# Products that nobody reads, in TensorE's waits between the phases of a two-layer kernel and in its last step

## The reference

```
xa = layer_norm(x);  sx = previous token - this token
xxx = tanh((xa + sx * maa_x) @ maa_w1), then five small products with maa_w2
xk, xw, xv, xr, xg = xa + sx * (maa_stack + xxx)
w = exp(-exp(time_decay + tanh(xw @ td_w1) @ td_w2))
r, k, v = xr @ Wr.T, xk @ Wk.T, xv @ Wv.T;  g = silu(xg @ Wg.T)
per token and head: out = r . (u * k v^T + s);  s = k v^T + w * s
x1 = x + group_norm(out) * g @ Wo.T
xc = layer_norm(x1), shifted and mixed into xk2 and xr2
result = x1 + sigmoid(xr2 @ Wfr.T) * (square(relu(xk2 @ Wfk.T)) @ Wfv.T)
```

## Time and profile before

| | before |
|---|---|
| median of three runs | 1484.47 us |
| the profiled execution, its own time | 1483.6 us |
| its span, first to last instruction | 1481.8 us |
| mean clock granted to TensorE | 0.973 of full speed |
| TensorE busy | 1388.5 us (94%) |
| VectorE busy | 888.9 us (60%) |
| ScalarE busy | 722.5 us (49%) |
| GpSimd busy | 486.7 us (33%) |

### The profile page before, as it was taken

One profiled execution on the slowest core, in us unless ns is written; L12 is line 12 of the kernel. 1 busy time (PEld: TensorE's weight loads), 2 busy tenths in 40 slices (PEclk: granted clock), 3 DMA queues, 4 the chain that ended last, 5 costly groups with the idle time before them and its releaser, 6 DMA issues. The chain is left out here.

```text
span 1481.8 us, 41201 instructions
## 1 busy us (share of the span) xinstructions
PE 1388.5 (94%) x16448; PEld 1007.6 (68%) x16448; DVE 888.9 (60%) x2287; ACT 722.5 (49%) x1772; POOL 486.7 (33%) x530
## 2 busy tenths in 40 slices
PE   5999999999999999947989999999999999999965
PEld 4777777777777777626766667666676666666632
DVE  3444444444444443433887788887878878787751
ACT  3666666666666666521245344443444434444422
POOL 2211111111111111011543456434554345543330
PEclk9999999999999999968899999999999999999997
DMA  7531111111111100012001000011000010010000
GB/s 217 152 92 41 41 41 40 39 39 39 39 38 35 34 24 14 7 32 105 11 20 27 27 20 9 25 26 26 19 10 26 26 27 8 20 26 21 20 13 6
DMA packets 25686, 54.97 MB, mean 37 GB/s; under 512 B 3984, under 2 KB 6672, under 8 KB 24016
## 3 DMA queue, kind: packets, MB, share of 16 engines
q1 hardware_dynamic: 25552, 52.99, 12.4%
HBM read 42.23 MB, written 7.34 MB: 33 GB/s over the span
## 5 line engine op out<-in xcount | busy, mean ns | idle before, releaser
L907 POOL TENSOR_TENSOR rst<-rp,st 128x448 f32<-128x448 f32 x192 | 193.9, 1029 | 74.4 <-DVE st L1105 49.7
L270 POOL TENSOR_TENSOR aT_lo<-whole,aT_hi 128x375 fp32r<-128x375 f32 x64 | 58.6, 916 | 443.9 <-ACT whole L422 441.1
L342 DVE CUSTOM_DVE_ANT_0 probs<-a_bank,unmask 112x375 f32<-112x375 f32 x256 | 126.0, 545 | 79.7 <-PE a_bank L539 72.4
L899 POOL TENSOR_TENSOR xm<-mixed,xa 128x448 f32<-128x448 f32 x80 | 87.8, 1097 | 240.6 <-DVE mixed L1034 239.1
L441 ACT ACTIVATE probs<-probs,least 112x375 f32<-112x375 f32 x256 | 153.8, 607 | 0.0
L348 DVE RECIPROCAL inv_rows<-sums 112x128 f32<-112x128 f32 x64 | 61.0, 953 | 153.9 <-ACT probs L441 153.9
L450 ACT COPY probsT<-a_bank 125x448 f32<-125x448 f32 x192 | 90.1, 535 | 51.7 <-PE a_bank L594 51.7
L1034 DVE SCALAR_TENSOR_TENSOR mixed<-b_bank,vec_sb,sx 128x112 f32<-128x112 f32 x320 | 83.1, 328 | 53.5 <-PE b_bank L1552 52.7
L594 PEld LDWEIGHTS a_bank<-ident_sb,probs 112*125 112x125 f32 x768 | 90.8, 188 | 30.9 <-ACT keyT L432 16.3
L594 PE MATMUL a_bank<-ident_sb,probs 112*125 112x112 f32 x768 | 99.3, 279 | 2.7 <-ACT probs L441 2.7
L537 PE MATMUL a_bank<-aT_hi,wk_lo 128*128 128x376 f32 x256 | 91.1, 356 | 1.7 <-issue 1.7
(11 more groups left out here) (167 smaller groups left out, 3100.0 us busy)
## 6 DMA issues: line engine op xcount, KB each, us to landing
ctx_tok<-in_ctx SPq DMA_DIRECT2D x16, 750.0 KB
xT_sb<-in_xT SPq DMA_DIRECT2D x16, 224.0 KB, 9.7
x_tok<-in_x SPq DMA_DIRECT2D x16, 224.0 KB, 9.4
x_between_layers<-x_sb SPq DMA_DIRECT2D x16, 224.0 KB, 2.3
b_x<-x_between_layers SPq DMA_DIRECT2D x16, 224.0 KB, 2.7
x_post<-x_between_layers SPq DMA_DIRECT2D x16, 224.0 KB, 2.8
out_dram<-fin SPq DMA_DIRECT2D x16, 224.0 KB, 2.3
vbd<-vtok SPq DMA_DIRECT2D x208, 16.0 KB
```

The lines of the kernel that those rows point to most:

```text
L342: dve.tensor_tensor_reduce(out=probs[:, g % 2, i], in0=score_bank[i][0:T, 0:TC], in1=unmask[:, m[1]], scale=-SCALE, scalar=-LOWEST, op0=AL ...
L899: pool.tensor_tensor(xm[:, f % 2], mixed[:, f % 2], xa[:, :, 1:T + 1], ALU.add).then_inc(s_xm, 1)
L907: pool.tensor_tensor(by_chunk(rst[:, j % NPROD]), by_chunk(rp[:].rearrange("p c t -> p (c t)")), state_of(j), ALU.mult).then_inc(s_pprod, 1)
```

## The change

It adds a helper to TensorE's stream. `keep_clock(dst, n)` runs n fp32 products of 128 rows and 512 columns: the identity as weights, the first block of layer 1's wv as the moving operand, into a PSUM bank whose content is not read. They carry no semaphore. It is called in seven places of `step`: 11 before the first transposes and 3 before `maa_first` in step 0, 5 before `transpose_keys` in step 1 and 4 in step 2, and in the last step 6 before `project_out`, 3 before `transpose_post` and 3 before `ffn_key`. Together that is 35 products. One wait, for the load of wv, is added at the beginning. Nothing is removed or moved.

```diff
--- before.py
+++ after.py
@@ -1506,6 +1506,11 @@
 
 
 
+            def keep_clock(dst, n):
+
+                for _ in range(n):
+                    pe.matmul(dst[:, 0:D], ident[:], W["wv"][:, 0], start=True, stop=True)
+
             def transpose_x(b):
                 pe.wait_ge(s_ln, count(b, 1, 1))
                 if at_least(b, 1):
@@ -1690,8 +1695,15 @@
             def step(n, pre, scans, post, first):
                 p, m, l, more = later(n, 1), later(n, -1), later(n, -2), pre and not is_batch(n, B - 1)
                 if first:
+                    pe.wait_ge(w_loaded["wv"], 16)
+                    keep_clock(post_bank[1], 11)
                     transpose_x(n)
+                    keep_clock(post_bank[1], 3)
                     maa_first(n)
+                if is_batch(m, 0):
+                    keep_clock(post_bank[1], 5)
+                elif is_batch(m, 1):
+                    keep_clock(post_bank[0], 4)
                 if scans:
                     transpose_keys(m)
                 if pre:
@@ -1724,6 +1736,8 @@
                     maa_second(n, (3, 4))
                 if scans:
                     attend_near(m, 3)
+                if is_batch(l, B - 1):
+                    keep_clock(pre_bank[0], 6)
                 if post:
                     project_out(l)
                 if more:
@@ -1732,8 +1746,12 @@
                     project(n, 3, "wr", s_rmm)
                 if scans:
                     reduce(m, 1)
+                if is_batch(l, B - 1):
+                    keep_clock(pre_bank[0], 3)
                 if post:
                     transpose_post(l)
+                if is_batch(l, B - 1):
+                    keep_clock(pre_bank[0], 3)
                 if pre:
                     project(n, 4, "wg", s_gmm)
                     transpose_value(n)
```

## The result

Six executions with the change gave 1475.10 to 1481.08 us, median 1477.55; six of the kernel before, 1482.65 to 1484.83, median 1483.06. The ratio is 0.9959, with a 95% interval of 0.9947 to 0.9970: faster by 0.4%, some 6 us. The forecast was 1470.3, and the measured median lies just above its range (1477.5). The direction was right and the size less than half of the 13.5 us forecast.

A forecast was written before the change was run, and what follows sets the result against it. TensorE was taken to bound the middle, with slow clock at both ends. Terms of 3.0, 2.8, 2.8 and 4.9 us summed to 13.5, off 1483.6 us: 1470.1, given as 1470.3; range 1465.5 to 1477.5.

The forecast's parts named there:

- The bound and the carry: From 760 to 1080 us TensorE is busy 318.9 of 320 us, so time won earlier should move all that follows.
- The first rival: Early gain lost as TensorE waits for VectorE or GpSimd, or clock falls, in steps 2, 3: 1478.7 us, chance 0.14.
- The last step: 6, 3 and 3 products fill three waits and hold the clock for the work behind each: 4.9 us won.
- Step 1: Five products in the 4.93 us wait for the chunk keys hold the clock behind it: 2.8 us won.
- Step 2: Four products in a wait of 4.73 us hold the clock in the 10.4 us behind it: 2.8 us won.
- The turn: Between the layers, 11 and 3 products hold the clock for the transposes and products behind them: 3.0 us won.
- The wait on the wv weights holds nothing: At the turn: load issued in layer 0's second step, hundreds of us before, so the added wait delays nothing.
- The overrun that was put at half of 0.7 us: At the turn: a low clock spell makes the 11 products end late, transposes 0.7 us late; 0.35 taken as lost.
- the 1.5 us put on the clock holding over the two short waits behind maa_first: At the turn: faster decay products and wv, +2.6 us if the clock holds, nothing if not; 1.5 taken.
- The second rival: Products with identity weights don't count as work for the clock, take 1.72 us each and overrun: 1507.5 us, chance 0.04.
- The third rival: Nothing comes of the change, as the slow stretches lie beside other waits: 1483.6 us, chance 0.03.
- The base: 13.5 us off the profiled execution's 1483.6 us gave 1470.1; with the runs' median 0.9 above it, 1470.3 was given.

The follow-up runs named there:

- the second profile of the change: The changed kernel run again unaltered, against the kernel before: 1477.19 us, ratio 0.9947.

## Why the prediction was wrong, point by point

- **The bound and the carry** were right. The 13 middle steps take 602.7 us with the change and 602.8 before, 602.0 to 605.1 in all profiles (602.0 to 604.1 without the one that leaves copies out), and so closely it can be said that what is won ahead of them is kept. The first rival expected new waits on VectorE or GpSimd behind the second step. There is one, in step 3, with the change; before, such a hole stood in step 4 (the two lines below). Step 3 takes 47.25 us for 46.29 before, step 4 46.29 for 47.17, so it is moved rather than added: TensorE's idle time in the 13 steps is 2.2 us with the change and 2.0 before. The rival's thought, that TensorE comes sooner and waits for something else, was right where it cost time, but for another engine's queue and as early as steps 1 and 2.

```profile
804.73 0.98 PE L1557 MATMUL b_bank<-th,b_maa 32*64 32x112 f32 x16 [0.89 <-DVE mixed L1034]
...
847.63 0.25 PE L1635 MATMUL b_bank<-vbd,kz 40*32 40x80 f32 x1 [0.62 <-issue]
```

- **The last step** was right in its mechanism and size: 4.9 forecast, and 5.2 from the output product to the end in every profile that has the 12 products, which is the prediction's full sum. The clock did not fall ahead of the first six products, for which the prediction had kept back 0.3 us.
- **Step 1** was right in size, 2.8 against 2.9 and 3.2, though not for certain: with the clock falling in the new wait it was 0.2.
- **Step 2** is one of the two terms that failed, by 7.4 us in the first profile and 2.9 to 3.1 in the three with four products, all the copies and a short spell (step 2 at 48.97, 49.12 and 49.24 us). The prediction took TensorE's busy 10.4 us behind the transposes as work that would shrink with the clock, with VectorE as the only thing that could be late next. Late next was the last of SyncE's 13 copies of the values, 1.2 us in each of the two steps. The wait costs 1.2 us itself, and it is an unfilled hole close behind the fill: in it, or right behind it, the clock fell in step 2 in both profiles of the change. Forecast were 2.8 us won; measured were 4.6 and 0.3 us lost. With six copies left out the step is 2.6 us shorter than before, so the size was right for a step without that wait.
- **The turn** is the other: 3.0 us forecast to be won, 0.4 and 0.5 lost. It failed at two steps. "The wait on the wv weights holds nothing" was true, but the 11 products behind it were not free: with them the load of x lands up to 1.8 us later (2.5 to between 3.1 and 4.3). The overrun that was put at half of 0.7 us was 0 in one profile, where instead the clock fell in the rest of the wait, and 0.9 in the other. And the 1.5 us put on the clock holding over the two short waits behind maa_first came to little, since in both profiles it fell there. With the load left alone and one of those waits filled, the turn is 2.8 us shorter, against 3.0 forecast.
- **The second rival** is refuted as it was put: in the last step the 12 records ahead of the last output product take 5.31 us, 0.43 each, so the clock was at 2.4 GHz with the identity as weights. In the eight products after the load it even rose while they ran (10.1 us in all, where 1.2 GHz throughout would be 13.8). Its mechanism, an overrun at 1.2 GHz, is real where the fill starts at 1.2 GHz, as the eight products after the load and the second profile of the change show.
- **The third rival** is refuted by the last step.
- **The base** of the forecast does not add up: 13.5 us from the median of 1484.47 is 1471.0, and 1470.3 was given. It is 0.7 us of the miss.
- **The range** was narrow against what the clock does by itself: the executions of one kernel, the changed one, spread over 6 to 7 us here. But the median missed by 7 us for the two terms above, and not for that spread. The rule cited from the Trainium skill (TensorE: Matmul & The Clock Gate, Part 1: The HAM clock gate), that the part of a kernel that runs slow varies from run to run, agrees with the six clocks of 0.984 to 0.992 of one program. It was cited and then not priced.

## What to carry to other kernels

Fill in TensorE's waits pays where one chain is the whole program, as in a last step: read the wait ahead of each product and fill it closely, at the price of the higher clock if the engine was just working. Here rests of 0.56 to 1.16 us kept the clock in the last step, and one of 2.25 us in the turn did not. Wherever a stretch gets faster, list all that it waits for, the DMA queue's issues among them, and check by how much each was early before: a wait that is hidden exactly is a new bound. And a fill that leaves a hole of a microsecond behind it may keep nothing.

## What had not been expected of the hardware

- A load of 224 KB landed 1.3 us later (3.9 for 2.6) where a 16 KB packet of instructions was fetched beside it. If the fetch is the cause, which is not shown, instructions that are on no critical path delay data that are.
- Length of idleness is a poor guide to the clock. It held over the wait of 2.21 us in step 0 in all twelve profiles (transposes of 0.57 us behind it), though in four of them it fell some 1 us after those began. And it fell in waits of 1.14 to 1.21 us in step 2, or (once) 0.2 us behind one, in each profile that had four products there and all the copies.
